# A decoder block on Trainium2: a new order for the cross-attention stage on TensorE, ScalarE and VectorE

## The reference

```
x = x + first_attn(layernorm(x))
q = layernorm(x) @ Wq.T + bq;  k = ctx @ Wk.T + bk;  v = ctx @ Wv.T + bv      # ctx: 128 rows for each sequence
p = softmax(where(mask, q k / sqrt(32), -1e8))                                 # 16 heads of 32 features
x = x + (p v) @ Wo.T + bo
s = layernorm(x) @ Win + bin                                                   # 64 values a token
h = relu(s[..., None] * W1 + b1);  g = sum(h * W2, -1) + b2                    # 16 hinges for each of the 64
x = x + g @ Wout + bout
```

## Time and profile before

| | us |
|---|---|
| median of 3 runs | 1888.51 |
| lowest, highest | 1885.15, 1889.79 |
| the profiled execution | 1890.52 |
| its span, first to last instruction | 1888.6 |
| busy: TensorE, VectorE, ScalarE, GpSimd | 1697.8, 1503.0, 1087.1, 1006.6 |
| cross stage, first scores of step 0 to those of step 15 | 898.65 to 1782.40 |

### The profile page before, as it was taken

The page is one execution under the profiler, slowest core; times in us unless marked ns, Lnnn a source line. Parts: engine busy times, 40 slices in busy tenths (PEclk is TensorE's granted clock), DMA queues, the critical chain, the costliest instruction groups (busy, mean ns, idle before and its releaser), DMA issues.

```text
span 1888.6 us, 38076 instructions
## 1 busy us (share of the span) xinstructions
PE 1697.8 (90%) x14016; PEld 1408.6 (75%) x14016; DVE 1503.0 (80%) x2108; ACT 1087.1 (58%) x3438; POOL 1006.6 (53%) x716
## 2 busy tenths in 40 slices
PE   4899999999999999945799999999999999999975
PEld 3678888888888888834677777777777777777764
DVE  5788888888888888761578888888888888888874
ACT  3434444444444444332777778777777777787761
POOL 3167777777777777653254446544465444654322
PEclk9999999999999999967799999999999999999987
DMA  5311111111111111042101212011110111201101
GB/s 196 88 58 39 45 46 45 45 45 45 45 45 45 45 45 46 23 100 75 42 2 53 59 59 64 18 59 59 59 64 19 59 59 59 65 18 59 36 18 45
DMA packets 72794, 98.76 MB, mean 52 GB/s; under 512 B 22208, under 2 KB 30528, under 8 KB 72640
## 3 DMA queue, kind: packets, MB, share of 16 engines
q1 hardware_dynamic: 70624, 94.25, 15.7%
q10 hardware_dynamic: 2016, 2.45, 0.4%
HBM read 59.66 MB, written 37.03 MB: 51 GB/s over the span
## 4 chain that ended last, share of the span: by engine, by line
PE 31%; DVE 10%; ACT 8%; issue 3%; POOL 1%; POOLq 0%; DVEq 0%; ACTq 0%
PE ring L1252 20%; ACT prob_c L1384 6%; PE sc L1280 4%; PE ring L1347 3%; DVE ntop L1456 3%; DVE x2T L1424 2%; PE ring L1257 2%; DVE pT L1424 2%; ACT x2T L1357 1%; PE sc L1272 1%; DVE stats L1463 1%; PE ring L1305 1%; DVE x L1477 1%; DVE q L1530 1%; ACT q L1357 1%
## 5 line engine op out<-in xcount | busy, mean ns | idle before, releaser
L404 PE MATMUL qb<-wqkv,xT 128*128 128x512 f32 x2304 | 551.0, 393 | 6.1 <-DVE wqkv L867 6.1
L404 PEld LDWEIGHTS qb<-wqkv,xT 128*128 128x128 f32 x2304 | 429.3, 189 | 93.4 <-DVE wqkv L867 6.3
L1384 ACT ACTIVATE prob_c<-sc,ntop 128x128 f32<-128x128 f32 x1024 | 361.4, 405 | 119.1 <-DVE ntop L1456 119.1
L1212 POOL TENSOR_TENSOR rstd<-vare,half_c 128x1 f32<-128x1 f32 x64 | 35.1, 549 | 502.3 <-DVE vare L1470 502.3
L1384 ACT ACTIVATION_READ_ACCUMULATOR prob_c<-sc,ntop 128x1 f32 x1024 | 251.0, 245 | 0.0
L1252 PE MATMUL ring<-wqkv,aT_c 128*128 128x512 f32 x768 | 198.3, 409 | 39.0 <-DVE x L1477 39.0
L324 POOL TENSOR_TENSOR prod_pool<-v,prob 128x1024 f32<-128x1024 f32 x64 | 180.6, 2822 | 77.3 <-DVE prob L793 71.4
L493 PE MATMUL ob<-wout,aT 128*128 128x512 f32 x768 | 192.7, 401 | 11.1 <-DVE aT L823 11.1
L1252 PEld LDWEIGHTS ring<-wqkv,aT_c 128*128 128x128 f32 x768 | 143.4, 193 | 73.6 <-issue 45.0
L573 ACT ACTIVATE v<-qb 128x512 f32<-128x512 f32 x64 | 38.3, 598 | 260.0 <-PE qb L404 251.6
L1252 PE MATMUL ring<-xT_c,wqkv 128*128 128x512 f32 x768 | 185.9, 402 | 1.4 <-DVE xT_c L1424 1.4
(11 more groups left out here) (137 smaller groups left out, 3335.2 us busy)
## 6 DMA issues: line engine op xcount, KB each, us to landing
x_tile<-in_x SPq DMA_DIRECT2D x16, 1024.0 KB, 5.2
x_scratch<-xres SPq DMA_DIRECT2D x16, 1024.0 KB, 4.5
x_tile<-x_scratch SPq DMA_DIRECT2D x16, 1024.0 KB, 6.9
out<-x SPq DMA_DIRECT2D x64, 256.0 KB, 2.0
kt<-k_scratch SPq DMA_DIRECT2D x16, 512.0 KB, 3.2
v_c<-v_scratch SPq DMA_DIRECT2D x16, 256.0 KB, 4.8
raw<-in_wqkv SPq DMA_DIRECT2D x3, 1024.0 KB, 6.7
ctx<-in_ctx SPq DMA_DIRECT2D x1, 1024.0 KB, 8.2
```

Of the source, the lines that this page charges most:

```text
L404: last = nc.tensor.matmul(qb[g % 4][:, :], xT[p][a][:, k, t * P:(t + 1) * P], wqkv[b][:, k, c * D:(c + 1) * D], start=(n == 0), stop=(n == ...
L1384: last = nc.scalar.activation(prob[:, h, :], sc[g][:, (h % 4) * C:(h % 4 + 1) * C], ACT.Exp, bias=ntop[:, h:h + 1], accum_out=total[:, t % ...
```

## The change

The order inside the cross stage is another on TensorE, ScalarE and VectorE; GpSimd and the DMA queue keep theirs. No matmul, exponential or eviction is added or removed but for `s`: one turn with 12 matmuls of 512 columns for two turns with 24 of 256, and one eviction of 512 columns for two of 256.

- TensorE: slot t is scores(t), `aT`, then the last two `pT` of the sub-tile before, `out`, `wo`, `xT`, `pv`, `x2T`, and the first two `pT` of its own. In slot 3 the turns after `pv` are `pT` 12 and 13, `s`, `x2T`, `q`, `pT` 14 and 15. `aT` transposes what the slot before divided.
- ScalarE: the last two `pT` of the sub-tile before are evicted between the first and the second group of exponentials, `xT` before the fourth, `pT` 14 and 15 at the start of the next step.
- VectorE: low parts and `out`'s sum stand between the reductions, one after each; the second layernorm's statistics follow directly on the sum they are of; `gT` is before `pT` 14 and 15.
- The bank follows from the turns that do happen, in a list over all steps (`RING`).

```
 def slot_turns(t):
...
+    turns = [("aT", t)]
+    if t > 0:
+        turns += [("pT", 4 * t - 2), ("pT", 4 * t - 1)]
+    turns += [("out", t), ("wo", t)]
     if t in (1, 2):
         turns += [("xT", 2 * t - 2), ("xT", 2 * t - 1)]
...
+    turns += [("pv", t)]
+    if t < 3:
+        return turns + [("x2T", t), ("pT", 4 * t), ("pT", 4 * t + 1)]
+    turns += [("pT", 12), ("pT", 13), ("s", 0), ("x2T", 3)]
+    return turns + [("q", m) for m in range(DK)] + [("pT", 14), ("pT", 15)]
...
-    "aT": lambda j, i: 4 * j + i,
+    "aT": lambda j, i: 4 * j + i - 1,
...
-    return (TURNS.index(turn) + 2 * parity) % 4
+RING = [(j, kind, i) for j in range(-1, TILES + 2) for kind, i in TURNS if active(j, kind, i)]
+PLACE = {turn: n for n, turn in enumerate(RING)}
...
+    return PLACE[(j, *turn)] % 4
...
+                prob_hi(j - 1, 14)
+                prob_hi(j - 1, 15)
+                attn_hi(0)
+                for g in range(4):
+                    exps(0, g)
+                for t in (1, 2, 3):
+                    norm2_hi(t - 1)
+                    prob_hi(j, 4 * t - 4)
+                    prob_hi(j, 4 * t - 3)
+                    attn_hi(t)
+                    exps(t, 0)
+                    prob_hi(j, 4 * t - 2)
+                    prob_hi(j, 4 * t - 1)
+                    exps(t, 1)
+                    exps(t, 2)
+                    if t < 3:
+                        norm_hi(2 * t - 2)
+                        norm_hi(2 * t - 1)
+                    exps(t, 3)
...
+                for t in (1, 2, 3):
+                    norm2_lo(t - 1)
+                    prob_lo(j, 4 * t - 4)
+                    tops(t, 0)
+                    prob_lo(j, 4 * t - 3)
+                    attn_lo(t)
+                    tops(t, 1)
+                    add_out(t)
+                    prob_lo(j, 4 * t - 2)
+                    tops(t, 2)
+                    prob_lo(j, 4 * t - 1)
+                    tops(t, 3)
+                    add_attn(t)
+                    statistics(t)
+                    if t < 3:
+                        norm_lo(2 * t - 2)
+                    normalise(t)
+                    if t < 3:
+                        norm_lo(2 * t - 1)
```

More of the change, by code:

```diff
@@ L1017 @@
     "q": lambda j, i: 4 * (j + 1) + i + 1,
[L1018 removed]
+    "s": lambda j, i: j,
     "out": lambda j, i: 4 * (j - 2) + i + 1,
@@ L1049, in bank_before @@
 def bank_before(j, turn):
[L1051 to L1061, removed]
+    at = PLACE[(j, *turn)] - 4
+    if at < 0:
+        return None
+    step, kind, i = RING[at]
+    return kind, TURNS_OVER[kind](step, i)
 def cross_block(nc, x1_dram, st_dram, scratch, w_in, b_in, out, keep):
@@ new lines, in prob_T, with attn_T @@
+                def prob_T(i):
+                    if not has(j):
+                        return
+                    g = i % 4
+                    wait(pe, exped, 16 * j + i + 1)
+                    dst = bank(j, p, ("pT", i))
+                    for h in range(4):
+                        last = nc.tensor.transpose(dst[:, h * P:(h + 1) * P], prob[:, 4 * g + h, :], ident[:, :])
+                    last.then_inc(psum["pT"], 1)
+                def attn_T(t):
+                    if not active(j, "aT", t):
+                        return
+                    wait(pe, taken["pv"], TURNS_OVER["aT"](j, t))
+                    transpose_tile(bank(j, p, ("aT", t)), attn).then_inc(psum["aT"], 1)
@@ L1350, in _ @@
+                ffn_in()
+                norm2_T(3)
+                for m in range(DK):
+                    queries(m)
+                prob_T(14)
+                prob_T(15)
             pe.wait_ge(k_zero, 1)
@@ new lines, in step @@
+                prob_hi(j, 12)
+                prob_hi(j, 13)
+                norm2_hi(3)
+                if is_step(j, -1):
+                    act.wait_ge(in_small, 16 * len(small))
+                if has(j, 1):
+                    wait(act, scored, 16 * (j + 1))
+                for m in range(DK):
+                    hinges(*HINGE_RUNS[m])
+                    if has(j, 1):
+                        take_hi(j, p, "q", m, q[0][:, m, :], ACT.Identity, bias=bq[:, m:m + 1])
+                if active(j, "s", 0):
+                    wait(act, hinged, PAIRS * j)
+                    wait(act, psum["out"], 4 * (j - 1))
+                    nc.scalar.activation(gT[0][:, :], g_sb[:, :], ACT.Copy).then_inc(g_hi, 1)
```

455 lines of the change are left out of this document (234 added, 221 removed).

## The result

The changed kernel takes 1875.39 us (median of 4 runs, 1873.4 to 1876.6), beside 1887.95 for the kernel before on the same chip (4 runs): ratio 0.9934, 95% interval 0.9916 to 0.9951. It is faster by 12.6 us, where 30.7 were forecast. 1875.39 lies in the range given (1834 to 1878), but at its far end, 17 us from 1858 and beside the 1874 of rival 2. What follows compares these two.

What follows compares the result with a forecast made beforehand. VectorE's chain was taken to bound slots 1 and 2. Savings of 16.1 us in thirteen middle steps, 4.4 in steps 0 and 1 and 10.2 in step 15 summed to 30.7, giving 1858 us, range 1834 to 1878.

Steps and rivals of the forecast that it cites:

- rival 2: Late ScalarE evictions cost 0.4 in slots 1 and 2 each; middle steps gain nothing, ends 14.6 us: 1874; chance 0.12.
- steps 0 and 1: First two steps, lacking `out`: 52.9 against 56.39 us and 56.5 against 57.40, 4.4 us saved together.
- step 15: Last step: the bank wait goes, slots 1 and 2 take 9.6 each, 8.2 less; with slot 0's 1.95, 10.2 us.
- the tail: From step 15's slots 1 and 2 to the end, 67.62 us: no change taken, bounds 3 us either way.
- The bound and the place of the waits: VectorE's order sets slots 1 and 2; its second low `xT` frees the last `pT`'s bank, TensorE idle about 1.0 us.
- Slots 1 and 2: Middle slots set by VectorE's chain from the first reduction to the second low `xT`: 11.7 us against 12.15.
- the waits here are for other engines that are mostly early: Reason for pricing VectorE's alternating reductions and low parts at 0.60, not 0.71, which would lengthen slots 1 and 2 by 1.0.
- no idle place between 1.82 and 10.4: VectorE's chain in slots 1 and 2 is unbroken between these times; argued against ScalarE's chain ending those slots.
- Slot 3: Slot with `s` and `q`: 12.28 to `q`, 12.21 to its last low part, 0.90 to scores; 25.4 us against 23.78.
- GpSimd hides too: GpSimd's 28.57 us a step keep their order and run beside the rest of slots 1 and 2 without lengthening them.
- Rival 4: TensorE's clock falls in slots 1 and 2, `wo` costs 1.6 more in each, 2.0 a step: 1899; chance 0.08.
- The dependent pair, 0.71: A VectorE instruction on 512 columns whose result the next awaits costs 0.71 us, against 0.60 for independent neighbours.

Runs made afterwards that it cites:

- experiment 3: Changed kernel with both low parts of `xT` ahead of reciprocal and division on VectorE in slots 1 and 2: 1847.61 us, ratio 0.9779.
- Experiment 4: Changed kernel with both low parts of `xT` ahead of the division, and the aggregation with its follower behind them too: 1838.16 us, ratio 0.9733.
- experiment 1: Kernel before the change with only the new bank list, banks following from turns that really happen: 1881.11 us, ratio 0.9957.
- Experiment 6: Changed kernel with ScalarE's two `pT` evictions ahead of the first group of exponentials instead of behind it: 1870.58 us, ratio 0.9903.
- Experiment 2: Changed kernel with VectorE's sum for `out` behind the last low `pT` of the sub-tile before, not ahead of the first: 1912.4 us, ratio 1.0137.
- experiment 7: Changed kernel with both parts of `gT` back behind `pT` 14 and 15 on ScalarE and VectorE: 1873.45 us, ratio 0.9916.
- experiment 8: Changed kernel with one more GpSimd wait: its work for the tile ahead begins only after VectorE's hinges of the step before: 1871.37 us, ratio 0.9909.

## Why the prediction was right and wrong

Of the 30.7 forecast, 17.2 came between the profiled executions. 9.9 are missing in the middle steps, 5.2 in steps 0 and 1, 0.35 in step 15; 0.8 came in the tail and 1.1 ahead of the stage, where none were forecast. That the total lies beside rival 2's 1874 is chance: rival 2 has nothing in the middle and 14.6 at the ends, and the runs have 6.2 and 11.0.

**The bound and the place of the waits: right.** VectorE's low parts of `xT` end slots 1 and 2, at a clock of 1.00, with TensorE idle 0.85 before the last `pT` (1.0 forecast). Experiments 3 and 4 show it best. Reciprocal and division are 0.88 of that chain (1325.15 to 1326.03), and taking them off shortens each slot by 0.89; with the aggregation and its follower (0.29) off too, it is 1.24.

**Step 15: right** (9.68 a slot, 9.6 forecast), and experiment 1 shows that 5.9 of the 8.1 are the bank list's; the rest is the order's.

**Slots 1 and 2, 11.7 forecast, 11.99 measured: the step that failed.** The walk had nine instructions at 0.60 from the first reduction on, all of them VectorE's own. Three of its links were longer:
- Low `aT` comes at 3.11, not 3.02, and low `pT` at 4.99, not 4.82. The step that I had dismissed is "the waits here are for other engines that are mostly early", and "no idle place between 1.82 and 10.4" was wrong by the walk's own prices: `aT` at 2.35, its eviction 0.55, four exponentials 1.37 and 0.63 to VectorE put that low `pT` at 4.90. In the trace, ScalarE's eviction of `aT` starts 0.76 behind TensorE's transposes, where I used the 0.63 of the earlier trace rows, and the four exponentials ahead of its `pT` make it late for VectorE. This is rival 2's mechanism, at the place that it names (low `pT` at 4.85). It costs 0.17, not the 0.4 that I gave it. Experiment 6 takes the exponentials out and gets 0.09 of it back; the other part comes with low `aT`.
- Statistics and aggregation add 0.03: the first low `xT` starts at 9.12, not 8.92, the second at 10.60, not 10.40.
- The last `pT` takes 0.56 up to the scores, not 0.43. The 0.43 was the distance of groups in an unbroken row; this one stands alone behind a wait.

0.17 + 0.03 + 0.13 makes 0.33 a slot (11.99 against the unrounded 11.66); the handover to TensorE was 0.83, as taken. The forecast had a gain of only 0.45 in such a slot, so an error of 3% of its length took most of it. With 0.2 more in slot 0, whose transposes also cost 0.48 a group where I took 0.43 and whose `wo` starts at 3.86, not 3.81, a step is 0.75 longer than the 58.0 forecast (which had rounded each slot up), and thirteen 10 us. That is what is missing in the middle.

**Slot 3, 25.4 forecast, 25.39 measured: right by luck.** `q` starts 12.21 into the slot (12.28 forecast), its last low part comes 12.38 behind that (12.21), and the scores 0.80 behind that (0.90). "GpSimd hides too" was true of GpSimd's own work and false of what it does to VectorE's.

**Steps 0 and 1, 4.4 forecast, -0.75 measured: the second step that failed.** "Steps 0 and 1 lack `out`" was costed at 0.60 a slot. Without the sum VectorE just waits 0.59 for the high `pT`, and step 1 has the same 11.99 as all others. Experiment 2 shows the other side of it. Step 0 is 2.9 longer than forecast, and most of that is the clock: its slot 2 takes 12.56 at a granted clock of 0.72, and 10.60 to 10.65 at 1.00 in experiments 7 and 8, which leave its order alone. There the clock falls in step 1 instead, which takes 62.4 to 62.5 in place of 58.75. So these two steps can't be compared to better than some 2 us.

**The tail, nothing forecast, 0.8 measured.** It hides two larger things: experiment 1 has 3.6 there from the list alone, and the first `out` behind the hinges starts 23.24 us behind slot 3's scores (1804.55 to 1827.79), where before it was 21.48 (1820.98 to 1842.46). I had `s` 2.4 us later and that paid back by `gT`; only part is. The first hinge starts 2.0 later (13.89 into the slot, not 11.86), and from there to the low `gT` it is 8.6 in place of 8.9, although the four low `pT` (2.4) no longer stand between: the hinges, with GpSimd beside them, take 1.4 longer, and VectorE waits 0.69 for the high `gT`. The tail's other steps were not tried one by one.

**Rival 4** (slower, 0.08) did not happen in the middle steps. Experiment 2 shows it 0.6 us away. By the Trainium skill (TensorE: Matmul & The Clock Gate, "A second HAM failure mode: psum-queue depth-cycling") short idle times between groups of matmuls that cycle through PSUM banks make the clock swing between its two levels. The changed kernel's middle steps don't show that, at a granted clock of 1.00; experiment 2 does, at 0.80 in the long slot.

**The dependent pair, 0.71.** Statistics 0.71 behind the sum and aggregation 0.73 behind the statistics, against 0.60 for neighbours that need nothing of each other: the price held. Experiment 4 shows what the wait itself is worth behind the statistics: there a low `xT` that needs nothing of them starts 0.65 behind (1307.20 to 1307.85). The Trainium skill (VectorE: DVE Perf Modes, "The DRAIN you can't avoid") says that a semaphore behind each instruction costs nothing extra. That is again not what the trace shows, with 0.71 and 0.73.

## What to carry to other kernels

When a loop is bound by a chain over several engines, walk each link with its own handover, from the first event to the last, and don't add up one engine's instructions: where the gain is a few per cent of the loop, 0.1 us on a link is a fifth of it (0.1 of 0.45 here). Then ask of each instruction on the chain whether the one behind it needs it. Here aggregation, reciprocal and division stood ahead of an eviction that needed none of them, and moving them back brought 37 us, three times what the whole reordering had. And when an engine's work slides in time without becoming more, look at what it now runs beside.

## What the runs showed of the hardware that I had not expected

- Some of VectorE's instructions that read SBUF alone slow down while GpSimd works on SBUF beside them: `scalar_tensor_tensor` on 128 x 512 f32 takes 750 ns alone and 1058 in the mean with GpSimd beside it part of the time (two in a row took 3.06 us at 1354.49), the subtraction for `gT` 692 against 1292, a `tensor_scalar` from SBUF 547 against 1096. In the same kernel low parts that read PSUM keep their 0.68 to 0.75, and so do the statistics, which read one tile in SBUF (0.69 at 1323.53, GpSimd busy from 1322.95 to 1325.11 but for 0.08). Two experiments turn it on and off by moving GpSimd alone. GpSimd's own instructions are slower there too: `xn_c` 1.48 beside the hinges, 1.04 elsewhere.
- TensorE's clock holds at 2.4 GHz in all 26 middle slots with idle times of 0.47 and 0.85 us and four transposes between them. With 1.05 and 0.85 it falls to 1.2 behind some slots and not behind others (12 of those 26 slots are longer than 12.59). Even the smaller pair isn't safe everywhere: in step 1, where TensorE also idles 0.60 ahead of `wo`, the clock falls behind 0.51 and 0.86 in experiment 8 and holds behind 0.51 and 0.85 in the changed kernel. Nothing in the kernel that runs at 1.00 tells how near it is.
- A group of four transposes costs 0.43 us in a row, 0.48 behind another kind of matmul, and 0.56 alone behind a wait.
